# Second layer of a two-layer mixture-of-experts program: from dense expert products over feature-major blocks to sorted tokens in tiles of 128 rows

## The reference, cut to what matters

```
x = x + 0.5 * L1_ffn(layernorm(x)); x = x + L1_attn(layernorm(x)); x = x + 0.5 * L1_ffn(layernorm(x))

L1_ffn:  scores = sigmoid(x @ gate_w)                     # 32 experts
         w, i   = top_k(scores, 6); w = w / sum(w)        # 6 experts for each token
         routed = sum over the 6: w * (silu(x @ wg[e]) * (x @ wu[e])) @ wd[e]      # width 96
         shared = silu(x @ sg) * (x @ su) @ sd                                      # width 192
L1_attn: Q, K, V = x @ W_in + b_in; rope on the first 128 features of Q and K
         A = sum over the sequence of K/|K| * V           # one vector of 256 for each sequence
         y = (A * Q) @ W_out + b_out
```

## Time and profile before

| what | us |
|---|---|
| median of 3 runs | 1899.73 |
| lowest and highest run | 1897.93, 1901.99 |
| profiled execution, first to last instruction (its span) | 1904.1 |
| of it: TensorE busy | 1733.1 (91%) |
| VectorE busy | 1136.4 (60%) |
| ScalarE busy | 701.5 (37%) |
| GpSimd busy | 183.6 (10%) |

### The profile page before, as it was taken

How to read it: one execution, slowest core, us unless ns; L and a number is a source line. 1 busy time by engine, 2 the same in 40 slices (tenths; PEclk the granted TensorE clock), 3 DMA queues, 4 the chain that set the end, 5 groups by cost and what they waited for, 6 DMA issues and landing times.

```text
span 1904.1 us, 21213 instructions
## 1 busy us (share of the span) xinstructions
PE 1733.1 (91%) x7604; PEld 1398.8 (73%) x7604; DVE 1136.4 (60%) x1817; ACT 701.5 (37%) x1038; POOL 183.6 (10%) x136
## 2 busy tenths in 40 slices
PE   4998888888988899999999999997659999999998
PEld 3776677676776778878888888885447878878787
DVE  4766576576466675675555555656567555455554
ACT  1334534544544343333333333333223333333332
POOL 7600000000000340350000000200004000000000
PEclk7999899998998999999999999998769999999999
DMA  5200000000000120120000000000001000000000
GB/s 168 67 1 1 1 0 0 0 0 0 0 0 0 58 67 0 34 75 1 0 1 0 0 0 0 23 1 23 33 2 42 1 11 0 0 11 0 12 1 11
DMA packets 14881, 30.65 MB, mean 16 GB/s; under 512 B 1648, under 2 KB 5872, under 8 KB 14832
## 3 DMA queue, kind: packets, MB, share of 16 engines
q1 hardware_dynamic: 14832, 30.01, 5.0%
HBM read 27.91 MB, written 2.10 MB: 16 GB/s over the span
## 4 chain that ended last, share of the span: by engine, by line
PE 74%; DVE 14%; issue 6%; ACT 5%; DMA 0%; DVEq 0%; SPq 0%; ACTq 0%
PE ps L345 47%; PE ps L415 19%; PE ps L358 3%; DVE HL L975 3%; PE ps L488 2%; DVE S L937 2%; PE ps L401 1%; ACT S L687 1%; DVE S L942 1%; DVE Cn L857 1%; PE ps L364 1%; ACT HL L693 1%; ACT L614 1%; ACT L687 1%; DVE OP L1004 1%
## 5 line engine op out<-in xcount | busy, mean ns | idle before, releaser
L345 PE MATMUL ps<-XN,W 128*128 (+1 forms) x4176 | 1022.6, 395 | 35.4 <-DVE XN L1004 11.5
L345 PEld LDWEIGHTS ps<-XN,W 128*128 128x128 f32 x4176 | 791.8, 191 | 211.2 <-DVE XN L861 13.6
L415 PE MATMUL ps<-HL,W 128*128 128x512 f32 x1920 | 505.9, 401 | 4.8 <-DVE HL L975 4.2
L937 DVE TENSOR_TENSOR S<-S,ps 128x512 f32<-128x512 f32 x320 | 219.6, 687 | 447.9 <-ACT S L687 446.1
L415 PEld LDWEIGHTS ps<-HL,W 128*128 128x128 f32 x1920 | 364.0, 191 | 95.1 <-DVE HL L975 11.5
L687 ACT ACTIVATE S<-ps 128x512 f32<-128x512 f32 x352 | 209.8, 597 | 582.8 <-PE ps L345 438.4
L975 DVE TENSOR_TENSOR HL<-S,HL 128x512 fp32r<-128x512 f32 x352 | 264.9, 754 | 115.1 <-ACT HL L693 108.1
L693 ACT ACTIVATE HL<-S 128x512 fp32r<-128x512 f32 x352 | 221.7, 631 | 285.9 <-PE ps L415 262.1
L942 DVE TENSOR_TENSOR S<-S,CB 128x512 f32<-128x512 f32 x280 | 208.0, 743 | 10.3
L331 POOL TENSOR_SCALAR W<-stage 128x768 fp32r<-128x768 f32 (+1 forms) x66 | 66.2, 1003 | 1266.8 <-DMA stage<-w 579.2
L333 POOL TENSOR_TENSOR W<-stage,W 128x768 fp32r<-128x768 f32 (+1 forms) x66 | 118.8, 1800 | 5.5
(11 more groups left out here) (135 smaller groups left out, 818.8 us busy)
## 6 DMA issues: line engine op xcount, KB each, us to landing
stage<-w SPq DMA_DIRECT2D x48, 384.0 KB, 3.0
stage<-wa SPq DMA_DIRECT2D x18, 256.0 KB, 2.6
x_raw<-x_in SPq DMA_DIRECT2D x1, 2048.0 KB, 8.3
CS<-cs SPq DMA_DIRECT2D x4, 512.0 KB, 3.3
out<-stage SPq DMA_DIRECT2D x4, 512.0 KB, 3.0
ident<-ident_in SPq DMA_DIRECT2D x1, 64.0 KB, 8.1
g<-gate SPq DMA_DIRECT2D x1, 32.0 KB, 5.7
vec<-vecs SPq DMA_DIRECT2D x1, 15.0 KB, 6.2
```

Of the source, the lines that this page charges most:

```text
L345: last = mm(dst, l, r, start=(n == 0), stop=(n == len(passes) - 1))
L415: last = mm(ps[:, YB + m, :], chunk_w(f, c, "down", part_w, m), HL[:, part_h, i % 2, :], start=(i == 0 and part_w == part_h), stop=(i == C ...
L937: tt(rows, rows, ps[:, GB + 2 * (i % 2) + 1, :], ALU.mult).then_inc(fs.prod, 1)
```

## The change

The first layer stays. In the second, each sequence of 1024 tokens is a stream. There are four passes through the expert block (2 sequences, before and after the attention), numbered `j` 0 to 3. For each pass the program

- takes the layer norm with the tokens on the partitions (`stats`, `scaled`), so the residual is now `XT`, token-major, and the normed tokens `xnt`;
- computes scores, the top 6, and on the chip a sort by expert: a cumulative count gives each of the 6 x 1024 (token, expert) pairs a row number in a buffer in DRAM in which every expert begins at a multiple of 128 rows (`chosen`, `slots`, `weights`). That buffer `xd` has `TILES` = 80 tiles of 128 rows, whatever the routing (48 full ones at least, and one more for each expert at most);
- scatters the normed rows to it by 48 indirect DMAs of 128 rows from GpSimd (`scatter`);
- runs 40 pairs of tiles (`tiles`), 160 pairs in the whole program. Each tile belongs to one expert, whose number TensorE's sequencer reads from SBUF (`next_experts`) and adds to the address of the weights. The products are plain float32, not split in parts;
- stores the result rows to `yd`, and gathers them by 48 indirect DMAs (`gather`), which VectorE adds to the residual with their weights (`gathered`), beside the tiles of the next pass where there is one;
- computes the shared branch with split operands (`shared`).

The attention (`attn`) is token-major as well. All 32 experts' weights lie unsplit in `WE`. `CUT` = 26 says after how many pairs of a pass the attention of the other sequence comes.

The diff, cut to what the prediction speaks of:

```diff

+PAIRS = TILES // 2
+ROWS = TILES * P
+assert ROWS % NTOK == 0
+BIG = 16384.0
+CUT = 26
+X_RING, Y_RING, G_RING = 4, 3, 6
+NG = ST * K1
 
 
 
 JOBS = 2 * NB
 B_ITEMS = L0.C + A0_HID
 
...
+            for g in range(E1 // 4):
+                sp.wait_ge(F0.down, LAST0 + -(-((g + 1) * 4 * EW) // SLOT))
+                sp.dma_start(WE[:, g * 4 * EW:(g + 1) * 4 * EW], w1[g]).then_inc(experts_in[g], 16)
...
+            def send(q):
+                i, j = q % PAIRS, q // PAIRS
+                sp.wait_ge(TL.y, q + 1)
+                sp.dma_start(pairs_of(yd[j])[i], yo[:, q % Y_RING]).then_inc(TL.sent[q % Y_RING], 16)
+
+            def tiles(q0, q1):
+                for q in range(q0, q1 + 2):
+                    if q < q1:
+                        i, j = q % PAIRS, q // PAIRS
+                        if i == 0:
+                            sp.wait_ge(scattered[j], 16 * NG)
+                        if q >= X_RING:
+                            sp.wait_ge(TL.turned, q - X_RING + 1)
+                        sp.dma_start(xd_in[:, q % X_RING], pairs_of(xd[FFN_STREAM[j]])[i]).then_inc(TL.landed[q % X_RING], 16)
+                    if q >= q0 + 2:
+                        send(q - 2)
+
+            tiles(0, PAIRS)
...
+            tiles(PAIRS + CUT, 2 * PAIRS)
+            tiles(2 * PAIRS, 2 * PAIRS + CUT)
+            tiles(2 * PAIRS + CUT, 3 * PAIRS)
+            tiles(3 * PAIRS, 4 * PAIRS)
+            rows_out = out.rearrange("(s t p) d -> s t p d", s=BATCH, p=P)
+            for s in range(BATCH):
+                for t in range(ST):
+                    sp.wait_ge(g_used, 2 * NG + s * NG + (t + 1) * K1)
+                    sp.dma_start(rows_out[s, t], XT[:, s, t, :]).then_inc(out_sent, 16)
+            sp.wait_ge(out_sent, 16 * BATCH * ST)
...
+            def scatter(j):
+                s = FFN_STREAM[j]
+                pool.wait_ge(filled[s], 16 * (ROWS // NTOK))
+                pool.wait_ge(RT.slots, j + 1)
+                pool.wait_ge(NM.xn, (FFN_NORM[j] + 1) * ST)
+                for t in range(ST):
+                    for k in range(K1):
+                        nc.gpsimd.indirect_dma_start(xd[s][:, :], bass.IndirectOffsetOnAxis(ap=slot_of[:, s, t, k:k + 1], axis=0),
+                                                     xnt[:, s, t, :], None).then_inc(scattered[j], 16)
+
+            def gather(j):
+                s = FFN_STREAM[j]
+                for i in range(Y_RING):
+                    pool.wait_ge(TL.sent[i], 16 * len(range(i, (j + 1) * PAIRS, Y_RING)))
+                for m in range(NG):
+                    t, k, n = m // K1, m % K1, j * NG + m
+                    if n >= G_RING:
+                        pool.wait_ge(g_used, n - G_RING + 1)
+                    nc.gpsimd.indirect_dma_start(G[:, n % G_RING, :], None, yd[j][:, :],
+                                                 bass.IndirectOffsetOnAxis(ap=slot_of[:, s, t, k:k + 1], axis=0)).then_inc(g_landed[n % G_RING], 16)
+
+            scatter(0)
+            scatter(1)
...
+            gather(0)
+            scatter(2)
+            gather(1)
+            scatter(3)
+            gather(2)
+            gather(3)
...
+                pe.load(regs[g], emap[0:1, FFN_STREAM[j], 2 * i:2 * i + 4])
+                for r in range(4):
+                    expert[2 * q + r] = pe.snap(regs[g][r], min_val=0, max_val=(E1 - 1) * EW)
...
+                def turned(q):
+                    pe.wait_ge(TL.landed[q % X_RING], 16 * (q // X_RING + 1))
+                    pe.wait_ge(TL.xT, q)
+                    for a in range(2):
+                        for k in range(KD):
+                            last = nc.tensor.transpose(ps[:, 0, (2 * a + k) * P:(2 * a + k + 1) * P],
+                                                       xd_in[:, q % X_RING, a, k * P:(k + 1) * P], ident[:, :])
+                    last.then_inc(TL.turned, 1)
+
+                def hturned(q):
+                    pe.wait_ge(TL.hid, q + 1)
+                    pe.wait_ge(TL.hT, q)
+                    for a in range(2):
+                        last = nc.tensor.transpose(ps[0:H1, 2, a * P:(a + 1) * P], hid[:, q % 2, a, :], ident[:, :])
+                    last.then_inc(TL.hturned, 1)
+
+                def up(q):
+                    i, j = q % PAIRS, q // PAIRS
+                    if i == 0:
+                        pe.wait_ge(RT.emap, j + 1)
+                    if q == 0:
+                        for g in range(E1 // 4):
+                            pe.wait_ge(experts_in[g], 16)
+                    if i % 2 == 0:
+                        next_experts(q)
+                    pe.wait_ge(TL.xT, q + 1)
+                    pe.wait_ge(TL.hid, q)
+                    for a in range(2):
+                        at = expert[2 * q + a]
+                        for k in range(KD):
+                            last = mm(ps[:, 1, a * 2 * H1:(a + 1) * 2 * H1], xT[:, q % 2, a, k, :],
+                                      WE[:, bass.ds(at + k * 2 * H1, 2 * H1)], start=(k == 0), stop=(k == KD - 1))
+                    last.then_inc(TL.gu, 1)
+
+                def down(q):
+                    pe.wait_ge(TL.hT, q + 1)
+                    pe.wait_ge(TL.y, q)
+                    for a in range(2):
+                        last = mm(ps[:, 3, a * D:(a + 1) * D], hT[0:H1, q % 2, a, :],
+                                  WE[0:H1, bass.ds(expert[2 * q + a] + 4 * H1, D)], start=True, stop=True)
+                    last.then_inc(TL.down, 1)
+
+                turned(q0)
+                for q in range(q0, q1):
+                    if q + 1 < q1:
+                        turned(q + 1)
+                    if q > q0:
+                        hturned(q - 1)
+                    up(q)
+                    if q > q0:
+                        down(q - 1)
+                hturned(q1 - 1)
+                down(q1 - 1)
+
...
+                    if t >= 2:
+                        pe.wait_ge(A1.rot, u - 1)
+                        pe.wait_ge(A1.kqv, u - 1)
+                    products(t)
+                    if t > 0:
+                        q_turned(t - 1)
+                q_turned(ST - 1)
...
+            slot(L0, F0, ("f0", order0), n, LAST0, n, 2 * NB + n, None, ahead)
+            pe.wait_ge(x_ready, 4 * NB)
+            convert(2)
+            convert(3)
+            shared(0)
+            norm(1)
+            route(1)
+            shared(1)
+            pe.wait_ge(SH.add, 4)
+            tiles(0, PAIRS)
+            tiles(PAIRS, PAIRS + CUT)
+            pe.wait_ge(TL.y, PAIRS + CUT)
+            norm(2)
+            attn(0)
+            norm(3)
+            route(2)
+            shared(2)
+            pe.wait_ge(SH.add, 6)
+            tiles(PAIRS + CUT, 2 * PAIRS)
+            tiles(2 * PAIRS, 2 * PAIRS + CUT)
+            pe.wait_ge(TL.y, 2 * PAIRS + CUT)
+            norm(4)
+            attn(1)
+            norm(5)
+            route(3)
+            shared(3)
+            pe.wait_ge(SH.add, 8)
+            tiles(2 * PAIRS + CUT, 3 * PAIRS)
+            tiles(3 * PAIRS, 4 * PAIRS)
...
+                def turned(q):
+                    act.wait_ge(TL.turned, q + 1)
+                    if q >= 2:
+                        act.wait_ge(TL.gu, q - 1)
+                    fn(xT[:, q % 2].rearrange("p a k t -> p (a k t)"), ps[:, 0, :], ACT.Copy).then_inc(TL.xT, 1)
+
+                def hturned(q):
+                    act.wait_ge(TL.hturned, q + 1)
+                    if q >= 2:
+                        act.wait_ge(TL.down, q - 1)
+                    fn(hT[0:H1, q % 2].rearrange("p a t -> p (a t)"), ps[0:H1, 2, 0:2 * P], ACT.Copy).then_inc(TL.hT, 1)
+
+                def gate(q):
+                    act.wait_ge(TL.gu, q + 1)
+                    fn(hid[:, q % 2], ps[:, 1, 0:4 * H1].rearrange("p (a u h) -> p a u h", a=2, u=2)[:, :, 0, :], ACT.Silu).then_inc(TL.silu, 1)
+
+                turned(q0)
+                for q in range(q0, q1):
+                    if q + 1 < q1:
+                        turned(q + 1)
+                    if q > q0:
+                        hturned(q - 1)
+                    gate(q)
...
+            def gathered(j, m):
+
+                s, t, k, n = FFN_STREAM[j], m // K1, m % K1, j * NG + m
+                if m == 0:
+                    dve.wait_ge(RT.wt, j + 1)
+                    dve.wait_ge(SH.add, 2 * j + 2)
+                dve.wait_ge(g_landed[n % G_RING], 16 * (n // G_RING + 1))
+                if k > 0:
+                    dve.wait_ge(g_used, n)
+                stt(XT[:, s, t, :], G[:, n % G_RING, :], wt[:, s, t, k:k + 1], XT[:, s, t, :], ALU.mult, ALU.add).then_inc(g_used, 1)
+
+            def tiles(q0, q1, beside=None):
+
+                def gated(q):
+                    dve.wait_ge(TL.silu, q + 1)
+                    tt(hid[:, q % 2], hid[:, q % 2], ps[:, 1, 0:4 * H1].rearrange("p (a u h) -> p a u h", a=2, u=2)[:, :, 1, :], ALU.mult).then_inc(TL.hid, 1)
+
+                def rows(q):
+                    dve.wait_ge(TL.down, q + 1)
```

(60 more changed lines are left out.)

990 lines of the change are left out of this document (682 added, 308 removed).

## The result

The changed kernel takes **2757.41 us** (median of 4 runs, 2747.46 to 2764.53) beside 1900.86 (4 runs) for the kernel before: 1.4495 times as long, 95% interval 1.4465 to 1.4525. Predicted were 2680, in a range of 2300 to 2950. The profiled execution spans 2759.6 us.

The account below looks back on a forecast made before the run. It took a closed chain of store, load and TensorE's work at lowered clock to bound the expert rounds: 160 x 8.9 = 1424 us, plus 1257 elsewhere, 2681, given as 2680 us, range 2300 to 2950.

Parts of the forecast that it names:

- What bounds the round: Expert tiles: each load waits behind an earlier pair's store, a closed chain of 8.9 us a round, 1424 us in all.
- far end of 9.8: Expert tiles: the round in us if TensorE always ran at half clock, 5.84 us of it work; 1568 us in all.
- The clock: Expert rounds: pauses of 3.9 us keep TensorE's clock low, work 1.7 times as long, 5.0 us; granted clock 0.5 to 0.7.
- rival of the full clock: Expert rounds: regular bursts keep TensorE's clock up, rounds of 6.9 us, 2361 us in total; chance 0.17.
- Work of a pair at the full clock: TensorE's transposes and products for one pair of tiles: 2.92 us.
- Expert numbers: TensorE's reads of them once in two rounds: taken as nothing, hidden under 0.65 us of transposes; at most about 2.6 us each.
- fixed stages: All outside the rounds: first layer 847, before the first tile 95, attention 240, last gathers and store 75; 1257 us.
- At half the clock in part of it 20 more; I leave that to the range: Second layer's attention, two streams at 240 us: a possible 20 us for low clock, not put in the sum.
- Indirect DMAs: GpSimd's scatters and gathers: 1.5 us each; scatters hidden, only the last 48 gathers and last store in the path, 75 us.
- rival of costlier transfers: Loads, stores and indirect DMAs share engines: rounds of 10.4 us, 3 us an indirect DMA, 3035 us; chance 0.11.
- faster rival: Expert rounds: loads run ahead after all, TensorE bounds rounds of 3.2 us at full clock, 1769 us; chance 0.15.
- break-even round of 4.0: Expert tiles: the round in us at which the changed kernel would equal the profiled 1904, given 1257 us outside the rounds.

Follow-up runs that it names:

- e1: Changed kernel with each store issued three pairs behind instead of two on SP's queue: 2069.81 us on chip B, 1.0869 of the kernel before.
- e2: Changed kernel with each store issued four pairs behind instead of two on SP's queue: 1964.75 us on chip B, 1.0336 of the kernel before.
- e3: Changed kernel plus 13 unused 128x512 products on TensorE at the end of each round: 2593.39 us on chip B, 1.3618 of the kernel before.
- e8: Same code as e2 (stores four pairs behind instead of two in the changed kernel), on chip A: 1850.10 us, 0.9752 of the kernel before.
- e4: Changed kernel with constants in place of the expert numbers TensorE reads, so no choice by routing: 2814.32 us on chip B.

## Why the prediction was right

- **What bounds the round.** Right by its mechanism and by every link. Predicted and measured in the round shown: copy 0.61 and 0.70; store's issue 0.38 and 0.36; load 2.6 and 2.89; TensorE 5.0 + 0.17 and 5.31 with the waits inside it; hops 0.2 and 0.12. The size is nearer to the far end of 9.8 than the mean of 8.94 shows. Twelve of the steps, two at the end of each of the six blocks of tiles, have no load ahead of them and take 2.1 to 2.6 us, 27.8 together; the 142 other rounds take 9.5. The prediction did not see the twelve. They took 79 us less than it gave them and the others 81 more, so that the mean of 8.94 lies on its 8.9 is luck. e1 and e2 show the order as the cause.
- **The clock.** Right: 0.69 over the rounds with their pauses and 0.56 over the work of the one shown; that work is 1.7 to 1.8 times as long as at the full clock (5.31 for 2.92 to 3.12), as taken from the bursts in the attention of before (1.7). The row of the third burst holds 16 of its 36 products, which took 9.90 us in all. The rival of the full clock fell; e3 shows that its condition was a filled pause. e3's round of 7.27 is above the 6.9 of that rival, mostly by the copy and the landing (0.70 and 2.87 for 0.61 and 2.6).
- **Work of a pair at the full clock,** 2.92 us: 2.82 and 3.12 by turns in e8, mean 2.97.
- **Expert numbers,** nothing: so it came in the rounds of this kernel (8.91 and 8.94), but not for the reason given. The 0.65 us of transposes were to cover a read; at half clock they take 1.54 and do, at the full clock, in e8, some 0.3 us of each read show. The floor of 600 ns a load that the Trainium skill gives on the page DMA: Bandwidth & Descriptors, section Latency and other measured facts, which would have added 0.3 us a round if none of it were covered, isn't seen in the rounds of this kernel, and e8 shows half of it in every second round. A floor bounds a load from below, so the "at most 48 us" of the prediction doesn't follow from it.
- **The fixed stages** carried the miss. Taken were 1257, and the profiled execution has 78.6 us more in all than the sum. The sum itself has a slip: its terms ahead of the first tile (11, 20 and 61) add to 92, less what overlaps, and it takes 95. Counting one round of 8.9 in each step between copies, the interludes are 33.5 and 29.7 too long, the breaks between blocks 4.3 and 4.4 (no term), the prelude 8.5; the other steps 5.9; the tail is 7.6 too short. The step that failed is "At half the clock in part of it 20 more; I leave that to the range": the attention runs at 0.63 and takes 77 us instead of 43, and 32 products of a single column in its sum take 7 us. I had priced these products at the full clock, from a stage of before that was dense, while the interlude is not. The clock isn't all of it: from 1583.30 to 1597.90 us the attention's products ran at 1.00, and seven of them took 2.02 us, where the prediction has 7 x 0.22 = 1.54. By that, an estimate, 8 tiles are 34 us at the full clock instead of 26, and the measured stretch of them is 49.8.
- **Indirect DMAs.** 1.5 taken; measured from one to the next 1.27 for the scatters (0.97 and a gap of 0.30), with a step of some 3.1 after every fourteen, and 1.25 for the last 48 gathers; the tail of these and the last store is 67 for 75. By the about 1 us to the first byte that the same page of the Trainium skill gives, those gathers would be 48 us; the trace has 1.25 each, 60. The prediction also turns the advice of the Trainium skill to join small transfers, in that page's section Rules for kernel authors, against transfers of 128 KB; the section speaks of sizes under 64 KB. The rival of costlier transfers didn't come: 10.4 us a round and 3 us a transfer were measured on no chip.
- **The faster rival,** 1769 at rounds of 3.2, was right about what a working prefetch gives: rounds of 3.04 in e8, 1850 with the fixed stages as they are. The ring of four input buffers was enough; the order kept it empty. A break-even round of 4.0 was too kind, by the fixed stages: 78 us more put it near 3.5, and e1's 4.1 (3.72 median) was slower than before, on B, which fits that.

So the sorted tiles did pay on the array (459 us of rounds in e8 for the 915 of the expert blocks before, which also hold the routing and the shared branch), and the change lost it to one closed loop of 9 us. With the stores issued two pairs later and TensorE kept busy in the interludes it takes 1819 us on chip A, 4.5% less than before; on chip C that is lost again, 0.5% more than before.

## What to carry to other kernels

On a queue that issues both loads and stores, walk the loop from a load back to itself: if a store ahead of it waits for the work that this load's predecessors feed, the ring of buffers stays empty and the period is the sum of the links; by the order of the program a deeper ring would not help, though no run here has one. Putting the store later, here by four pairs instead of two, cost nothing in the rounds of e8. Price the work between such pauses at the clock that the nearest paused stretch shows, in the small stages too. And a worst-case tile count is paid in full rounds, so count the empty ones before the change is written. What costs nothing under a pause can cost something once the pause is gone: here the reads of the expert numbers, and what differs between the chips.

## What was unexpected in the hardware

- The same kernel took 1850.10 on one chip and 1964.75 on another, 1819.18 and 1913.16, where the kernel before differed by 0.1%. Most of the loss on C (70.7 of 95 us) lies in dense rounds beside GpSimd's indirect transfers; on B 54 of 112 us lie in the rounds and 39 ahead of the first copy (e2 and e8, profiled executions). Engines stand for up to 8 us with nothing in the trace that they wait for. What it is inside the chip no run shows. A verdict near 1 for such a kernel needs more than one chip.
- Unused products made a kernel faster: 13 in each of 154 rounds of e3 gave 164 us against 2757.41 and 221 against e4 on the same chip; TensorE's part of a round went from 5.31 to 3.06 us, by the clock alone.
